# Second attention: a stack with mask rows of its own for the row maxima, in place of mask products

## The chip, the cores and the metric

The program runs on one core of a Trainium2 chip. The metric is the device time of one execution, in microseconds. The kernel before took 1235.64 us, the median of three runs (1232.64 to 1238.71).

## The reference, cut to what matters

x has 4 batches of 1024 tokens and 256 channels. Four stages add to it: an attention over 77 context rows, a gated mixture with a log, a second attention over the same context rows, and a self attention over 1024 keys in two classes. Only the third is touched:

```
n = layernorm(x)
q = n.reshape(4, 1024, 16, 16) @ Wq.T          # 16 heads of 16
k = ctx.reshape(4, 77, 16, 16) @ Wk.T
energy = einsum('bqhd,bkhd->bhqk', q, k)
energy = where(mask, energy, -1e20)            # mask: 1024 x 77, the same for all batches and heads
attn = softmax(energy / 4)                     # over the 77 keys
x = x + tanh(g) * ((attn @ v) @ Wo.T + bo)
```

The softmax needs the largest energy of each query row. The kernel computes it ahead of the scores, in a product of its own.

## The kernel before, in words

The second attention is cut into 16 units: unit u is batch u // 4 and heads 4 (u % 4) to 4 (u % 4) + 3, with 1024 tokens. A unit has two half units (m = 2u and 2u + 1) of 512 tokens, a half unit four steps (j = 0 to 3).

Precision comes from splitting queries and keys into three bf16 parts (high, middle, low). Chunks of 512 normalised tokens are split on chip and written to DRAM (`x_parts`, `write_half`, `write_parts`); then SP loads them back as a stack: 16 rows (the 16 channels of a head) for each pair of parts, 6 pairs, so 96 rows, for four heads and 1024 tokens. One such load (L553) has 128 KB, 16 rows x 4 x 1024; a unit has six. Keys are stacked the same way (`K1s`, L540). A product of stack and key stack is then the sum over all six pairs of parts.

For each unit:

- `max_product1` (L1424 to L1429) makes, for 128 queries at a time (eight per unit), the energies of four heads against 77 keys: first one mask product (L1424, the mask `mb1` against `I4`, 308 columns), then four small products of 96 rows and 77 columns (L1426). VectorE takes the negated maximum over the keys (L2028). The products use two banks in turn, so product n waits for the reduction of n - 2.
- `max_transposes1` (L1439) turns the maxima into a row; ScalarE (L1065) and GpSimd (`max_rows1`, L833) copy it under the stack as rows 96 to 99.
- `scores1` (L1459, L1460) makes keys x 512 tokens for one head, with the maxima subtracted by these rows, and adds the mask by a second product. ScalarE takes the exponential (L1085).
- `values1` (L1468) multiplies with the values, ScalarE copies (L1071), TensorE transposes back (L1477), VectorE divides (`normalise1`, L2047 and L2050).

The order is written out by hand. Step j of the scores of unit u stands behind the maxima product of unit u + 1 for the same j. So unit u + 1's stack must have landed when unit u's scores begin. In eight half units (m = 4, 6, ... 18) a half chunk of tokens is also transposed (L1380), cast by ScalarE (L1027), and its residue taken by VectorE (L1996) between two pairs of reductions; GpSimd makes the last part (L823, L825). Chunks 4 to 7 are written to `x_parts` (L545) while units 5, 7, 9 and 11 are loaded.

All transfers are issued by SP, in one queue. `load_x_stack(u)` waits until the scores of unit u - 3 are done, since three stacks are kept in turn; units 4, 8 and 12 (first of a batch) also wait until the chunks of their batch have landed in DRAM.

VectorE makes the mask `mb1` (L2005, 77 keys x 1024 tokens) from its bytes during the second stage.

Of the kernel before, what the change touches and what calls it, by code (L numbers as in the profile page):

```python
# [12 lines left out]
BF16 = mybir.dt.bfloat16  # L13
# [25 lines left out]
def build_program(nc, ins, out):  # L39
    ctx = ExitStack()  # L40
    with ctx:
# [177 lines left out]
        def parts_of(c):  # L219
# [3 lines left out]
        Xs = [v.bitcast(BF16).rearrange("p (j n) -> p j n", j=4)  # L223
              for v in (R4[0:SR1, 0:2048], R5[0:SR1, 0:2048], R5[0:SR1, 2048:4096])]
# [41 lines left out]
        STACK_DMAS = 6  # L266
# [161 lines left out]
        QM_ORDER, KM_ORDER, CLS_ROW, MROWS = (0, 0, 1), (0, 1, 0), 48, 50  # L428
# [72 lines left out]
        def _(sp):  # L501
# [36 lines left out]
            sp.dma_start(M1u, ins["mask1T"]).then_inc(s_m1, 16)  # L538
            for n, p in enumerate(K_ORDER):
                sp.dma_start(K1s[16 * n:16 * n + 16],  # L540
                             KXP[p].rearrange("(h d) n -> d h n", d=D)).then_inc(s_k1s, 16)
# [6 lines left out]
            def load_x_stack(u):  # L548
                b, hg = u // 4, u % 4
                if u >= 3:  # L550
                    sp.wait_ge(s_sc, 8 * (u - 2))
                for n, p in enumerate(Q_ORDER):
                    sp.dma_start(Xs[u % 3][16 * n:16 * n + 16],  # L553
                                 XP[p, 64 * hg:64 * hg + 64, S * b:S * b + S]
                                 .rearrange("(j d) t -> d j t", d=D)).then_inc(s_xs[u % 3], 16)
# [8 lines left out]
            sp.wait_ge(s_kw, 48)  # L564
            load_x_stack(0)
            sp.wait_ge(s_pl, 4)
            for c in range(2):
                write_half(c, 1, s_pw[c])
            for u in range(1, UNITS):
                b = u // 4  # L570
                if u % 4 == 0 or u == 2:
                    sp.wait_ge(s_pw[0], 16 * (b + 1))
                    sp.wait_ge(s_pw[1], 16 * (b + 1))
                load_x_stack(u)
                for c in WRITES.get(u, ()):
                    write_parts(c)
# [177 lines left out]
        def _(pool):  # L754
# [55 lines left out]
            pool.wait_ge(s_v1m, 8)  # L810
            pool.wait_ge(s_w1, 16 * 28)
# [17 lines left out]
            def max_rows1(m):  # L829
# [3 lines left out]
                pool.tensor_copy(Xs[m // 2 % 3][SR:SR1, :, 512 * (m % 2):512 * (m % 2) + 512],  # L833
# [15 lines left out]
            for m in range(2 * UNITS):  # L849
# [5 lines left out]
                if m + 2 < 2 * UNITS:  # L855
                    max_rows1(m + 2)
                if m == 9:
                    ln_rstd(2, [3])
                    pool.wait_ge(s_rs, 2 * 3 * B)
# [332 lines left out]
        def _(pe):  # L1192
# [218 lines left out]
            pe.wait_ge(s_k1s, 16 * STACK_DMAS)  # L1411
            pe.wait_ge(s_v1m, 8)
            pe.wait_ge(s_mk1, 1)
# [29 lines left out]
            def scores1(m):  # L1443
                u, q = m // 2, m % 2
                b, hg = u // 4, u % 4
                pe.wait_ge(s_mrc, m + 1)
                for j in range(4):
# [11 lines left out]
                    pe.matmul(o, K1s[:, 4 * hg + j, KX * b:KX * b + KX], Xs[u % 3][:, j, t], start=True, stop=False)  # L1459
# [355 lines left out]
        def _(dve):  # L1815
# [189 lines left out]
            dve.tensor_scalar(mb1, M1u, -1.0, BIG, ALU.add, ALU.mult).then_inc(s_mk1, 1)  # L2005
            add_log(2)
# [47 lines left out]
            for n in range(4, FIRST):  # L2054
                residue(n, bank(n))
            maxima1(1)
            dve.wait_ge(s_x2, NC)
            for m in range(2 * UNITS):
# [3 lines left out]
                if m in CHUNKS:  # L2062
                    ln_chunks(2, [CHUNKS[m]], lambda c: None)
                if m in STATS:
# [309 lines left out]
```

## Time and profile before

| | |
|---|---|
| median of 3 runs | 1235.64 us |
| profiled execution | 1233.77 us |
| its span | 1232.0 us |
| mean granted TensorE clock | 0.982 |
| TensorE, VectorE, ScalarE, GpSimd busy | 95%, 79%, 66%, 21% |
| 16 DMA engines busy (queue q1) | 39.6% |

The span is the time from the first to the last instruction of the profiled execution. The second attention takes from about 188 to 348 us of it; the self attention takes most of the rest. A busy TensorE counts matmuls that overlap, so starts tell more than durations. In a timeline a row merges neighbours of one kind: x4 means four of them, and the time in brackets is idleness just before, with what ended it.

### The profile page before, as it was taken

What the parts mean: (1) busy time and instruction counts of PE and PEld (TensorE: products, weight loads), DVE (VectorE), ACT (ScalarE), POOL (GpSimd) and SP (SyncE); (2) the same over time, 40 slices, a digit from 0 to 9 for tenths busy, and PEclk for the clock granted to TensorE, in tenths of its full rate; (3) what the DMA queues carried; (4) which work ended last, traced back from release to release, by engine and by line L of the source; (5) the groups of instructions that cost most, each with busy time, mean ns of one, the idle gap of its engine ahead of it and who ended that gap; (6) DMA issues with size and microseconds to landing.
All of it is one profiled execution on the core that took longest, in us unless ns stands there. A gap on an engine that the chain in (4) does not pass through costs nothing.

```text
span 1232.0 us, 26174 instructions
## 1 busy us (share of the span) xinstructions
PE 1164.6 (95%) x10391; PEld 534.3 (43%) x10391; DVE 973.2 (79%) x1431; ACT 818.4 (66%) x1471; POOL 258.3 (21%) x200
## 2 busy tenths in 40 slices
PE   5899999999998999789999999999999999999997
PEld 3577675555576456333322332332232323333345
DVE  6995587665447659688999999999999999999902
ACT  3234576777732743228888888888888888888871
POOL 3131345656632423540000000100100001001000
PEclk9978999999999999979999999999999999999999
DMA  6000336665300334751543454445534545364014
GB/s 208 25 1 17 34 78 149 108 130 104 52 27 13 116 128 120 148 77 46 91 71 71 98 98 68 90 77 94 85 79 91 98 76 92 66 100 81 12 44 142
DMA packets 89993, 101.73 MB, mean 83 GB/s; under 512 B 22154, under 2 KB 60300, under 8 KB 89872
## 3 DMA queue, kind: packets, MB, share of 16 engines
q1 hardware_dynamic: 89872, 100.06, 39.6%
q8 instruction: 83, 1.36, 0.5%
q14 instruction: 38, 0.31, 0.1%
HBM read 71.47 MB, written 24.33 MB: 78 GB/s over the span
## 4 chain that ended last, share of the span: by engine, by line
PE 60%; DVE 31%; ACT 4%; issue 2%; DMA 1%; SPq 1%; POOL 0%; POOLq 0%; ACTq 0%; DVEq 0%
DVE sm L2257 23%; PE ps L1705 11%; PE ps L1696 9%; PE ps L1683 7%; PE ps L1468 3%; PE ps L1565 3%; PE ps L1459 2%; PE ps L1460 2%; PE ps L1766 2%; PE ps L1524 2%; PE ps L1477 1%; PE ps L1426 1%; PE ps L1424 1%; ACT W L1162 1%; PE ps L1289 1%
## 5 line engine op out<-in xcount | busy, mean ns | idle before, releaser
L2257 DVE TENSOR_REDUCE sm<-ps 128x1 f32<-128x1024 f32 x512 | 601.8, 1218 | 34.8 <-PE ps L1683 30.6
L1162 ACT ACTIVATE W<-ps 128x512 f32<-128x512 f32 x1024 | 534.9, 603 | 122.6 <-PE ps L1705 120.2
L1705 PE MATMUL ps<-R 99*32 99x512 bf16 x4096 | 317.6, 384 | 0.9
L1696 PE MATMUL ps<-W,R 128*32 128x512 f32 x2048 | 265.4, 594 | 0.0
L1705 PEld LDWEIGHTS ps<-R 99*32 99x32 bf16 x4096 | 85.0, 94 | 203.6 <-ACT W L1162 156.1
L1683 PE MATMUL ps<-R 50*128 50x512 bf16 x512 | 91.6, 394 | 11.8 <-DVE sm L2257 7.5
L1683 PE MATMUL ps<-KM,R 50*128 50x512 bf16 x512 | 88.7, 384 | 5.1 <-DVE sm L2257 0.2
L1085 ACT ACTIVATE R<-ps 77x512 f32<-77x512 f32 x128 | 75.2, 593 | 20.6 <-PE ps L1460 11.3
L904 POOL COPY R<-R 128x512 f32<-128x512 f32 x16 | 9.8, 613 | 371.6 <-PE ps L1696 371.6
L1696 PEld LDWEIGHTS ps<-W,R 128*32 128x32 f32 x2048 | 63.0, 111 | 45.8 <-issue 0.5
L833 POOL COPY R<-R 4x2048 bf16<-4x2048 bf16 x32 | 60.5, 1892 | 57.0 <-ACT R L1065 49.0
L2028 DVE TENSOR_REDUCE small<-ps 128x4 bf16<-128x308 f32 x128 | 57.2, 472 | 13.3 <-PE ps L1426 13.3
L923 POOL TENSOR_TENSOR R<-R,W 128x512 f32<-128x512 f32 x8 | 10.3, 1282 | 268.0 <-DMA W<-sum_factors 268.0
L1683 PEld LDWEIGHTS ps<-R 50*128 50x128 bf16 x512 | 23.3, 93 | 98.6 <-issue 58.4
L1683 PEld LDWEIGHTS ps<-KM,R 50*128 50x128 bf16 x512 | 23.3, 93 | 95.7 <-issue 64.8
L1565 PE MATMUL ps<-R,W 128*128 128x512 f32 x128 | 58.5, 600 | 0.0
L1459 PE MATMUL ps<-R 100*77 100x512 bf16 x128 | 49.0, 383 | 0.0
L1460 PE MATMUL ps<-R 77*77 77x512 bf16 x128 | 48.6, 380 | 0.0
L1841 DVE TENSOR_SCALAR XN<-X,mv,rstd 128x256 f32<-128x256 f32 x128 | 47.0, 433 | 1.0 <-PE ps L1228 0.7
L2047 DVE RECIPROCAL small<-ps 128x16 f32<-128x16 f32 x32 | 8.2, 258 | 42.4 <-PE ps L1477 42.4
L1426 PEld LDWEIGHTS ps<-R 96*128 96x128 bf16 x512 | 33.9, 97 | 12.4
L1426 PE MATMUL ps<-R 96*128 96x77 bf16 x512 | 38.9, 198 | 0.0
(261 smaller groups left out, 1466.9 us busy)
## 6 DMA issues: line engine op xcount, KB each, us to landing
R<-x_parts SPq DMA_DIRECT2D x96, 128.0 KB, 4.6
R<-q_parts SPq DMA_DIRECT2D x192, 64.0 KB
R<-q_parts SPq DMA_DIRECT2D x96, 128.0 KB
R<-k_parts SPq DMA_DIRECT2D x96, 128.0 KB
q_parts<-R SPq DMA_DIRECT2D x24, 256.0 KB, 2.6
k_parts<-R SPq DMA_DIRECT2D x24, 256.0 KB, 2.7
x_parts<-R SPq DMA_DIRECT2D x6, 768.0 KB, 4.2
X<-in_x SPq DMA_DIRECT2D x4, 1024.0 KB, 10.2
```

What stands on the lines that cost most here:

```text
L833: pool.tensor_copy(Xs[m // 2 % 3][SR:SR1, :, 512 * (m % 2):512 * (m % 2) + 512], mrow1[:, m % 2].unsqueeze(1).to_broadcast([4, 4, 512])).t ...
L1085: act.activation(P1[:, m % 2, j, :], score_bank1(n)[0:KX, :], ACT.Exp, scale=0.25).then_inc(s_e1, 1)
L1162: act.activation(PR[:, s % 2, h, :], third_bank("score", 64 * u + n), ACT.Exp, scale=0.25).then_inc(s_sfree, 1)
L1426: mm = pe.matmul(o[:, KX * j:KX * j + KX], Xs[u % 3][0:SR, j, P * q:P * q + P], K1s[0:SR, 4 * hg + j, KX * b:KX * b + KX], start=False, st ...
L1459: pe.matmul(o, K1s[:, 4 * hg + j, KX * b:KX * b + KX], Xs[u % 3][:, j, t], start=True, stop=False)
L1460: pe.matmul(o, I4[:, 0:KX], mb1[:, t], start=False, stop=True).then_inc(s_sc, 1)
L1565: mm = pe.matmul(o[:, 512 * j:512 * j + 512], wqkv[:, i, C * kind + P * j:C * kind + P * j + P], XNT3[:, i, 512 * c:512 * c + 512], start= ...
L1683: mm = pe.matmul(pl[:, 512 * i:512 * i + 512], QMH[j][h][v, P * q:P * q + P], KM[j][v, h, :], start=True, stop=True)
L1696: mm = pe.matmul(bank(7)[32 * h:32 * h + 32, :], VST[j][:, k, h, :], PR[:, s % 2, h, :], start=(k == 0), stop=(k == TB - 1))
L1705: mm = pe.matmul(o[32 * c:32 * c + 32, :], KST[j][0:MAX_ROW + 1, h, t:t + 32], QST[j][0:MAX_ROW + 1, h, 512 * (s // 8):512 * (s // 8) + 51 ...
L2028: dve.tensor_reduce(Mn[:, u % 2, q, :], bank(n % 2)[:, 0:4 * KX].rearrange("p (j n) -> p j n", j=4), AX, ALU.max, negate=True).then_inc(s_ ...
L2257: dve.tensor_reduce(MX[:, half, h, q:q + 1], bank(2 * ((p + 1) % 2), 2), AX, ALU.max).then_inc(s_tfree, 1)
```

## The change

The maxima get stacks and key stacks of their own. A maxima stack has 125 rows: 77 mask rows (`mb1`, repeated for four heads) and 3 x 16 part rows, for the part pairs (0,0), (0,1) and (1,0) instead of all six. The maxima's key stack has a 77 x 77 identity over the key parts. One product of 125 rows then holds both mask and energies, and the product with `I4` is gone. The scores keep their stack of 96 + 4 rows.

The mask rows stay in place while part rows below them are loaded anew: even units use one buffer, odd units another (units 13 and 15 a third), so VectorE writes the mask rows three times (`mask_rows1`). GpSimd writes the identity four times (`preset_max_keys1`). SP loads three part groups per unit ahead of the six of the scores, three key groups per batch, and the wait counts change (`group_loads`).

```
+        def group_loads(g):
+            return 16 * sum((MAX_DMAS if n < UNITS else 0) + (STACK_DMAS if n else 0) for n in range(g % 3, g + 1, 3))
...
+            load_max_keys1(0)
             for n, p in enumerate(K_ORDER):
                 sp.dma_start(K1s[16 * n:16 * n + 16],
...
+            def load_max_stack1(u):
+                b, hg = u // 4, u % 4
+                if u == 2:
+                    sp.wait_ge(s_mp, 8)
+                if u >= 3:
+                    sp.wait_ge(s_sc, 8 * (u - 2))
+                if u == 13:
+                    sp.wait_ge(s_pl, 2 * NC)
+                for n, p in enumerate(QM_ORDER):
+                    sp.dma_start(max_stack1(u)[KX + 16 * n:KX + 16 * n + 16],
                                  XP[p, 64 * hg:64 * hg + 64, S * b:S * b + S]
                                  .rearrange("(j d) t -> d j t", d=D)).then_inc(s_xs[u % 3], 16)
...
+            load_max_stack1(0)
             load_x_stack(0)
+            sp.wait_ge(s_dl, NC)
+            load_max_stack1(1)
...
             for u in range(1, UNITS):
                 b = u // 4
                 if u % 4 == 0 or u == 2:
                     sp.wait_ge(s_pw[0], 16 * (b + 1))
                     sp.wait_ge(s_pw[1], 16 * (b + 1))
+                if u >= 2:
+                    load_max_stack1(u)
                 load_x_stack(u)
+                if u == 2:
+                    sp.wait_ge(s_k1s, 16 * (MAX_DMAS + STACK_DMAS))
+                    for n in range(1, B):
+                        load_max_keys1(n)
                 for c in WRITES.get(u, ()):
                     write_parts(c)
...
             def max_product1(u, qs):
                 b, hg = u // 4, u % 4
-                pe.wait_ge(s_xs[u % 3], 16 * STACK_DMAS * (u // 3 + 1))
+                pe.wait_ge(s_xs[u % 3], group_loads(u))
+                pe.wait_ge(s_mk1, 4 if u >= 13 else 3 if u >= 1 else 2)
+                if b >= 1:
+                    pe.wait_ge(s_k1s, 16 * (MAX_DMAS * B + STACK_DMAS))
+                    pe.wait_ge(s_v1m, 9 + b)
                 for q in qs:
                     n = 8 * u + q
                     if n >= 2:
                         pe.wait_ge(s_mr, n - 1)
                     o = bank(n % 2)[:, 0:4 * KX]
-                    pe.matmul(o, mb1[:, P * q:P * q + P], I4, start=True, stop=False, skip_group_check=True)
                     for j in range(4):
-                        mm = pe.matmul(o[:, KX * j:KX * j + KX], Xs[u % 3][0:SR, j, P * q:P * q + P],
-                                       K1s[0:SR, 4 * hg + j, KX * b:KX * b + KX], start=False, stop=True,
+                        mm = pe.matmul(o[:, KX * j:KX * j + KX], max_stack1(u)[:, j, P * q:P * q + P],
+                                       max_keys1(b)[:, 4 * hg + j, :], start=(j == 0), stop=True,
                                        skip_group_check=True)
...
+            def mask_rows1(u):
+                dve.tensor_copy(max_stack1(u)[0:KX], mb1.unsqueeze(1).to_broadcast([KX, 4, S])).then_inc(s_mk1, 1)
+
+            dve.wait_ge(s_mk1, 1)
+            dve.wait_ge(s_kw, 16)
+            mask_rows1(0)
```

The load of the scores' stack now waits on the semaphore of the next unit's group (`s_xs[(u + 1) % 3]`), so the maxima products of a unit wait for their own three loads and for the six of the unit before.

TensorE, one half unit of the second attention without a transposed half, before (L1424 is the mask product, L1426 the small ones, L1459 and L1460 the scores):

```order
187 L1424 MATMUL ps<-R 128x308
188 L1426 MATMUL ps<-R 128x77 x4
189 L1459 MATMUL ps<-R 77x512
190 L1460 MATMUL ps<-R 77x512
191 L1424 MATMUL ps<-R 128x308
192 L1426 MATMUL ps<-R 128x77 x4
193 L1459 MATMUL ps<-R 77x512
194 L1460 MATMUL ps<-R 77x512
```

The same place after (L1490 the small products, L1525 and L1526 the scores):

```order
147 L1490 MATMUL ps<-R 128x77 x4
148 L1525 MATMUL ps<-R 77x512
149 L1526 MATMUL ps<-R 77x512
150 L1490 MATMUL ps<-R 128x77 x4
151 L1525 MATMUL ps<-R 77x512
152 L1526 MATMUL ps<-R 77x512
```

The products of 308 columns are gone; nothing else moved there. SP's queue from the first stack on, before (L553 loads for the scores' stack, L558 and L545 writes of parts):

```order
29 L558 DMA x_parts<-R 128x3x512 x2
30 L553 DMA R<-x_parts 16x4x1024 x6
31 L558 DMA x_parts<-R 128x3x512 x2
32 L553 DMA R<-x_parts 16x4x1024 x12
33 L545 DMA x_parts<-R 128x6x512 x2
34 L553 DMA R<-x_parts 16x4x1024 x18
35 L545 DMA x_parts<-R 128x6x512
```

And after (L594 loads for the maxima's stack, L581 for the scores', L562 keys of the maxima, L599 and L573 writes):

```order
30 L599 DMA x_parts<-R 128x3x512 x2
31 L594 DMA R<-x_parts 16x4x1024 x3
32 L581 DMA R<-x_parts 16x4x1024 x6
33 L594 DMA R<-x_parts 16x4x1024 x3
34 L599 DMA x_parts<-R 128x3x512 x2
35 L581 DMA R<-x_parts 16x4x1024 x6
36 L594 DMA R<-x_parts 16x4x1024 x3
37 L581 DMA R<-x_parts 16x4x1024 x6
38 L562 DMA W<-ctx_key_parts 16x16x77 x9
39 L573 DMA x_parts<-R 128x6x512 x2
40 L594 DMA R<-x_parts 16x4x1024 x3
```

Every unit now has nine stack loads. Unit 2's three maxima loads and nine key loads stand ahead of the writes of chunks 2 and 3. VectorE, at the mask and before the first maxima, after (L2071 makes the mask, L2074 is the new copy, L2101 the reductions, L2062 the residues):

```order
102 L2034 TENSOR_TENSOR R<-R 128x1024
103 L2071 TENSOR_SCALAR R<-R 77x1024
104 L2074 COPY R<-R 77x4096
105 L2039 SCALAR_TENSOR_TENSOR X<-R,gates,X 128x1024
...
122 L2101 TENSOR_REDUCE small<-ps 128x4 x4
123 L2062 TENSOR_TENSOR R<-ps,R 128x512 x4
124 L2074 COPY R<-R 77x4096
125 L2101 TENSOR_REDUCE small<-ps 128x4 x8
```

The copies are new; their neighbours stand as before.

## Rows read from the trace of the kernel before

**Rows 1.** The page, busy time of the engines.
```profile
PE 1164.6 (95%) x10391; PEld 534.3 (43%) x10391; DVE 973.2 (79%) x1431; ACT 818.4 (66%) x1471; POOL 258.3 (21%) x200
```

**Rows 2.** Chain of waits in order of time, 278 to 310: start us, us, what.
```profile
279.39 0.99 PE ps L1468 x8
...
284.48 1.00 PE ps L1468 x8
...
289.15 1.00 PE ps L1468 x8
```

**Rows 3.** Timeline of TensorE where unit 2's scores begin.
```profile
211.95 0.30 PE L1424 MATMUL ps<-R 77*128 77x308 bf16 x1
212.09 0.30 PE L1426 MATMUL ps<-R 96*128 96x77 bf16 x4
```

**Rows 4.** Loads of one stack line L553, units 8 and 9, each by itself.
```profile
L553 SPq DMA_DIRECT2D R<-x_parts x6: 302/426/427, 253.2 to 255.4; - x6
DMA to landing us min/median/max: 3.2/4.7/6.0
...
L553 SPq DMA_DIRECT2D R<-x_parts x6: 302/427/1734, 259.2 to 262.7; - x6
DMA to landing us min/median/max: 3.3/4.2/4.6
```

**Rows 5.** Windows: span, busy of each engine, clock, DMA share, GB/s.
```profile
302.50:304.50 2.00, 2.00 (x21) 0.81 (x20) 0.52 (x2) 1.45 (x3) 1.94 (x2) 1.00 1.04 124
190.00:192.00 2.00, 1.61 (x18) 1.06 (x19) 2.00 (x4) 1.16 (x3) 0.48 (x1) 1.00 1.04 182
```

**Rows 6.** Timeline, first maxima product of unit 8.
```profile
261.51 0.29 PE L1424 MATMUL ps<-R 77*128 77x308 bf16 x1 [0.53 <-issue]
```

**Rows 7.** Timeline, outputs' transposes, first reductions, third mask product of a half unit.
```profile
304.33 0.65 PE L1477 MATMUL ps<-identF,R 128*128 128x128 f32 x4
...
305.65 0.85 DVE L2028 TENSOR_REDUCE small<-ps 128x4 bf16<-128x308 f32 x2
...
306.27 0.29 PE L1424 MATMUL ps<-R 77*128 77x308 bf16 x1
```

**Rows 8.** Timeline, end of a half unit with a transposed half.
```profile
274.60 0.85 DVE L2028 TENSOR_REDUCE small<-ps 128x4 bf16<-128x308 f32 x2
...
275.51 0.24 PEld L1439 LDWEIGHTS ps<-identB,small 128*4 128x4 bf16 x4 [0.70 <-DVE small L2028]
```

**Rows 9.** Groups by line and form, VectorE: busy us, mean ns.
```profile
L1928 DVE CAST R<-small 128x3072 bf16<-128x3072 f32 x1 | 1.8, 1761 | 0.0
```

**Rows 10.** Timeline of VectorE, behind the mask and at unit 0's last reductions.
```profile
158.04 1.28 DVE L1973 SCALAR_TENSOR_TENSOR X<-R,gates,X 128x1024 f32<-128x1024 f32 x1 [0.52 <-ACT R L1017]
...
193.73 0.86 DVE L2028 TENSOR_REDUCE small<-ps 128x4 bf16<-128x308 f32 x2 [0.23 <-PE ps L1426]
```

**Rows 11.** Timeline of TensorE, beginnings of the scores of units 0 and 15.
```profile
194.97 0.30 PE L1424 MATMUL ps<-R 77*128 77x308 bf16 x1
...
337.55 0.38 PE L1459 MATMUL ps<-R 100*77 100x512 bf16 x1
```

**Rows 12.** Writes of chunks 2 and 3 (L545): issue to landing.
```profile
DMA to landing us min/median/max: 4.2/4.2/4.2
```

**Rows 13.** Loads of the key stack, line L540.
```profile
L540 SPq DMA_DIRECT2D R<-ctx_key_parts x6: 330/448/449, 140.6 to 142.9; - x6
DMA to landing us min/median/max: 3.4/5.8/7.6
```

**Rows 14.** Windows around a stop of TensorE after the second attention.
```profile
396.00:399.00 3.00, 0.82 (x8) 0.00 (x0) 3.00 (x5) 1.93 (x3) 2.13 (x1) 1.00 0.00 0
399.00:402.50 3.50, 3.01 (x10) 2.43 (x11) 3.50 (x7) 1.90 (x3) 0.00 (x0) 0.52 0.65 225
```

**Rows 15.** Loads of unit 2's stack (L553), issued behind others.
```profile
L553 SPq DMA_DIRECT2D R<-x_parts x6: 303/424/557, 186.5 to 188.8; - x6
DMA to landing us min/median/max: 3.6/4.5/4.9
```

More of the change, by code:

```diff
@@ L222, in build_program, with x_stack, max_stack1, max_keys1 @@
         xres = R4[:, 2048:4096].rearrange("p (u j n) -> p u j n", u=2, j=2)
-        Xs = [v.bitcast(BF16).rearrange("p (j n) -> p j n", j=4)
-              for v in (R4[0:SR1, 0:2048], R5[0:SR1, 0:2048], R5[0:SR1, 2048:4096])]
+        QM_ORDER, KM_ORDER = (0, 0, 1), (0, 1, 0)
+        def x_stack(u):
+            v = (R4[0:SR1, 0:2048], R5[0:SR1, 0:2048], R1[0:SR1, 4096:6144] if u == 2 else R2f[0:SR1, 0:2048])[u % 3]
+            return v.bitcast(BF16).rearrange("p (j n) -> p j n", j=4)
+        MAXR = KX + 48
+        def max_stack1(u):
+            v = R5[0:MAXR, 2048:4096] if u % 2 == 0 else R1[0:MAXR, 6144:8192] if u < 12 else R4[0:MAXR, 2048:4096]
+            return v.bitcast(BF16).rearrange("p (j n) -> p j n", j=4)
+        def max_keys1(b):
+            v = R2f[0:MAXR, 7482:8098] if b == 0 else W[0:MAXR, 2048 + 616 * b:2664 + 616 * b]
+            return v.bitcast(BF16).rearrange("p (h n) -> p h n", h=H)
         On = R1[:, :].rearrange("p (i c) -> p i c", i=NT)
@@ L538, in _, with load_max_keys1 @@
             sp.dma_start(M1u, ins["mask1T"]).then_inc(s_m1, 16)
+            def load_max_keys1(b):
+                for n, p in enumerate(KM_ORDER):
+                    sp.dma_start(max_keys1(b)[KX + 16 * n:KX + 16 * n + 16],
+                                 KXP[p].rearrange("(h d) n -> d h n", d=D)[:, :, KX * b:KX * b + KX]
+                                 ).then_inc(s_k1s, 16)
+            load_max_keys1(0)
             for n, p in enumerate(K_ORDER):
@@ L810, in _, with preset_max_keys1 @@
             pool.wait_ge(s_v1m, 8)
+            def preset_max_keys1(b):
+                pool.tensor_copy(max_keys1(b)[0:KX], identB[0:KX, 0:KX].unsqueeze(1).to_broadcast([KX, H, KX])
+                                 ).then_inc(s_v1m, 1)
+            preset_max_keys1(0)
             pool.wait_ge(s_w1, 16 * 28)
@@ L832, in max_rows1 @@
                     pool.wait_ge(s_sc, 4 * (m - 5))
-                pool.tensor_copy(Xs[m // 2 % 3][SR:SR1, :, 512 * (m % 2):512 * (m % 2) + 512],
+                if m == 10:
+                    for n in range(2):
+                        pool.wait_ge(s_pw[n], 32)
+                pool.tensor_copy(x_stack(m // 2)[SR:SR1, :, 512 * (m % 2):512 * (m % 2) + 512],
                                  mrow1[:, m % 2].unsqueeze(1).to_broadcast([4, 4, 512])).then_inc(s_mrc, 1)
@@ L856, in _ @@
                     max_rows1(m + 2)
+                if m in (1, 3, 4):
+                    pool.wait_ge(s_dl, NC)
+                    preset_max_keys1((m + 1) // 2 if m < 4 else 3)
                 if m == 9:
@@ L1410, in _ @@
             keep_warm(3, 4)
[L1411 to L1413 removed]
+            pe.wait_ge(s_k1s, 16 * (MAX_DMAS + STACK_DMAS))
+            pe.wait_ge(s_v1m, 9)
             pe.wait_ge(s_v1c, 2)
@@ L1446, in scores1 @@
                 pe.wait_ge(s_mrc, m + 1)
+                if u + 1 == UNITS:
+                    pe.wait_ge(s_xs[UNITS % 3], group_loads(UNITS))
                 for j in range(4):
@@ L1457, in scores1 @@
                     t = slice(512 * q, 512 * q + 512)
-                    pe.matmul(o, K1s[:, 4 * hg + j, KX * b:KX * b + KX], Xs[u % 3][:, j, t], start=True, stop=False)
+                    pe.matmul(o, K1s[:, 4 * hg + j, KX * b:KX * b + KX], x_stack(u)[:, j, t], start=True, stop=False)
                     pe.matmul(o, I4[:, 0:KX], mb1[:, t], start=False, stop=True).then_inc(s_sc, 1)
@@ L2055, in _ @@
                 residue(n, bank(n))
+            dve.wait_ge(s_dl, NC)
+            mask_rows1(1)
             maxima1(1)
@@ L2063, in _ @@
                     ln_chunks(2, [CHUNKS[m]], lambda c: None)
+                if m == 21:
+                    dve.wait_ge(s_pl, 2 * NC)
+                    mask_rows1(13)
                 if m in STATS:
```

8 lines of the change are left out of this document (5 added, 3 removed).

## The prediction

> **What bounds the kernel now.** I read the page first: TensorE is busy 95% of the span [rows 1], and about 150 of its 1232.0 us are the second attention, the only stage that the change touches. Then the chain of waits in order of time over that stage. It runs through TensorE alone: the value products (L1468) that close a half unit start 5.09 us apart where a half of 512 tokens is transposed inside the half unit, and 4.67 us apart where none is [rows 2]. So here a column less on TensorE is time saved, as long as nothing else becomes late. The timeline of TensorE gives the price of a mask product: L1424 starts at 211.95, the first small product behind it at 212.09 [rows 3]: 0.14 us, though its own duration is 0.30 (it is pipelined). There are 128 of them: 128 x 0.14 = 17.9 us is the most that their removal can return.
>
> The views of the transfers come last, and they decide. The six loads of unit 8's query stack are issued from 253.2 to 255.4; the first lands 3.2 us after its issue (256.4), the last 6.0 us after its own (261.4) [rows 4]. Five loads in 5.0 us: 1.0 us for each load of 128 KB, though SP issues one every 0.45 us. Unit 9's six are issued from 259.2 to 262.7 and have landed by 267.3 [rows 4]: twelve loads, still 1.0 us each. In such a stretch the 16 DMA engines are busy all the time (share 1.04) at only 124 GB/s [rows 5]. A unit of two half units has 6 us of such loads in 9.35 us, so they hide; with nine it has 9. And the queue is late once already: TensorE starts the first mask product of unit 8 at 261.51, after 0.53 us of idleness [rows 6], just behind the landing at 261.4. That is the wait that grows.
>
> **Removed.** The 128 mask products. In a half unit without a transposed half, the fourfold gain of 0.14 (0.56 us) is not got in full. VectorE normalises first: transposes of the outputs at 304.33, first reduction at 305.65 (+1.32), 0.47 long, and the third product of the half unit waits for its bank: +1.85. TensorE comes there at +1.94 now (306.27) [rows 7], and would come at +1.65. So it waits 0.2 us there, and the gain is 0.35. With a transposed half inside, the chain transposes, ScalarE cast, VectorE residue, two reductions has no slack even now: the reductions end at 275.45 (274.60 + 0.85) and the next loads of TensorE follow at 275.51 [rows 8]. That chain starts only 0.28 us earlier and then queues behind ScalarE's exponentials; I take 0.15. Over half units 0 to 29: eight at 0.15, nineteen at 0.35, the first three at about 0.5: 9.4 us. The units of the maxima then last 9.3 us (units 2 to 9) and 8.7 us (from 10).
>
> **Added, before the first unit.** VectorE writes 77 mask rows of 4096 bf16 elements three times. No row shows such a copy. The cast of L1928 takes 1.76 us for 3072 elements [rows 9], 0.57 ns each: 2.35 us is the upper end. It moves 6 bytes an element and the copy 4; by bytes it is 1.57, which I take; were it twice as fast as the cast, 1.2. The first copy stands between L2005 and L1973, where VectorE is idle 0.52 us [rows 10]; what follows to the start of the stage is one chain of VectorE, ScalarE and TensorE, so 1.05 us is lost. The second stands before the reductions that the last two products of unit 0 wait for: 1.57. The prologue's own products give back 0.3. The third, late in unit 10, fits VectorE's idle time. Scores begin at 194.97 now [rows 11], then at 197.3. [...] GpSimd's four presets of 77 x 1232 elements fall into its idle time.
>
> **Added, in SP's queue.** Three loads more a unit, of the same form and size (16 rows x 4 x 1024). They stand ahead of the six, and SP issues them when the unit three before has been scored. Also nine loads of key parts (39 KB each) ahead of the writes of chunks 2 and 3. The writes of parts stand behind the loads of their unit as before, and at units 4, 8 and 12 SP waits until the writes have landed before it loads anything. Prices:
> a load 1.0 us; its landing after an idle queue 3.2 (so 2.2 of start). A write of 768 KB lands 4.2 us after its issue [rows 12]: 2.0 of its own beyond the start; I take 2.5, since it stands behind loads. Key loads: the nearest row is the key stack, 154 KB in packets of 616 B: first landing 3.4 after 140.6, last 7.6 after 142.9 [rows 13], so 1.3 us each. By bytes a quarter of it, 0.33; by number of packets (the same 256), 1.3. I take 0.33, as they queue behind loads that are already issued: 3.0 for nine.
>
> The ledger, in the trace's time. Unit 0's last product ends near 194.0 now (the last pair of its reductions starts at 193.73 [rows 10]), at 196.4 then; its buffer is unit 2's, so SP issues unit 2's maxima stack only then: landed 196.4 + 2.2 + 3 = 201.6 (needed 204). Unit 2's query stack 207.6, keys 210.6, two writes 215.6, unit 3's maxima stack 218.6. Its products stand in unit 2's scores, which begin at 211.95 now [rows 3] and could begin at 212.5: **a stop of 6.1 us**. It is the largest single term. From then on the beginnings of the units are the later of TensorE's (the one before + 9.3 or 8.7) and of the queue's: unit 3 227.9 (TensorE), 4 237.2 (TensorE), 5 248.1 (queue, behind write 4), 6 257.4, 7 270.8 (queue: unit 7's loads end at 263.1, write 5 at 265.6, then 5.2 for unit 8's maxima stack), 8 280.1, 9 291.3 (queue), 10 300.6, 11 314.0 (queue, behind write 7), 12 323.0, 13 332.0, 14 341.0 (all queue, 9 loads each), 15 349.6. Unit 15 begins at 337.55 now [rows 11]. So **the stage ends 12.0 us later**: 9.4 gained, 2.3 paid before it, 19.3 in new waits for loads (6.1 at unit 2, 4.1 and 4.7 at units 7 and 11, the rest 1.6, 1.9 and three of 0.3).
>
> [...]
>
> [...]
>
> **Sum.** The profiled execution took 1233.77 us. 1233.8 + 12.0 = **1245.8 us**. The median of the three runs (1235.64) lies 1.9 above it, within their own spread of 6; I don't add it.
>
> **Rivals.**
> 1. Loads that pack. The six loads issued from 186.5 to 188.8 land between 3.6 and 4.9 after issue (190.1 to 193.7) [rows 15], 0.73 us each, at 182 GB/s [rows 5]; others were queued ahead of them, writes too. Were all like this, unit 2 would begin at 215.4 (stop 2.9), no later unit would wait, and unit 15 would begin at 215.4 + 8 x 9.3 + 5 x 8.7 = 333.3: 4.3 us gained, **1229.5**. Against it: units 8 and 9, twelve loads in a row at 1.0 us [rows 4]. Between the two ends (12.0 us later at 1.0, 4.3 earlier at 0.73) the sign turns near 0.88 us a load. Chance 0.13.
> 2. Halfway, 0.9 us a load. By the same ledger only unit 2 (stop 4.9) and units 7 and 11 (1.2 and 2.9) wait: unit 15 begins 1.7 us later than now, **1235.5**. Chance 0.22.
> 3. Small packets and writes cost more: keys 1.3 each (+8.7 at unit 2, whose delay the full queue passes on): **1254.5**. Chance 0.13.
> 4. The change does what it says on TensorE; the order of instructions shows the mask products gone.
> My forecast: 0.52, its own range 1240 to 1253.
>
> Half a percent, 6.2 us, is about what a measurement can tell. Slower by more (over 1241.8): most of the forecast (0.49), rival 3 and a little of rival 2: 0.64. Faster by more (under 1229.5): half of rival 1 and a part more if VectorE's waits are smaller than I think: 0.10. The same: 0.26. Range: 1230 to 1256.
>
> **What would show it.** In the timeline of the changed kernel: TensorE idle 5 to 7 us at the first product of unit 3; waits of 2 to 5 us where units 8 and 12 are first needed; landings still 1.0 us apart and DMA share near 1 in the whole stage; units of 9.0 us at its end. Wrong if the landings come 0.75 apart, if the steps without a transposed half go down to 4.1 us, or if TensorE is busy throughout.

## The result and the profile after

The changed kernel took 1250.12 us, the median of 13 runs (1245.86 to 1253.76); the kernel before took 1236.76 us in 13 runs beside it (1232.3 to 1244.44). The ratio is 1.0099, 95% interval 1.0081 to 1.0116, so 12.2 us slower (10.0 to 14.3). The forecast was 12.0 us slower. As a time it was 1245.8, 4.3 below the median, since the 12.0 were added to a single execution of 1233.8. The difference is right; the runs below show that it came out right from parts of which several were wrong.

The profiled execution of the changed kernel took 1250.54 us, 16.8 more than the one of before. So differences between these two traces are 3 to 5 us larger than those between medians; most of that is found below (the clock at 37 to 44 us).

The page, busy time of the engines; it answers to [rows 1]:

```profile
PE 1162.0 (93%) x10263; PEld 528.0 (42%) x10263; DVE 984.3 (79%) x1434; ACT 816.2 (65%) x1471; POOL 267.8 (21%) x204
```

TensorE has 128 instructions fewer and waits more. The chain of waits in order of time, the value products that close a half unit (start us, us, what), answers to [rows 2]:

```profile
278.38 1.00 PE ps L1534 x8
...
283.01 0.99 PE ps L1534 x8
...
287.60 0.99 PE ps L1534 x8
```

4.63 and 4.59 us, where before it was 4.67 and 5.09: a unit is 0.55 us shorter. And the chain stays on TensorE: here no wait for a load. The timeline of TensorE (start us, us, what, in brackets the idle time just before) has two stops and no third:

```profile
227.06 0.42 PE L1490 MATMUL ps<-R 125*128 125x77 bf16 x4 [7.60 <-issue]
...
316.98 0.31 PE L1490 MATMUL ps<-W,R 125*128 125x77 bf16 x4 [3.69 <-DVE small L2101]
```

The first is the forecast one: unit 3's first product, inside unit 2's scores ([rows 3] is that place before). It waits for unit 3's maxima stack, issued from 217.1, the last part landed at 227.0. The second was not forecast. It stands in unit 11's scores, at the products for unit 12, and belongs to VectorE, whose third copy is at the end of its own half unit 21, in unit 10. VectorE and GpSimd at that time:

```profile
310.23 4.52 POOL L926 TENSOR_TENSOR X<-X,bo 128x2048 f32<-128x2048 f32 x1
310.31 5.52 DVE L2074 COPY R<-R 77x4096 bf16<-77x4096 bf16 x1
...
314.80 2.77 POOL L892 COPY R<-R 4x2048 bf16<-4x2048 bf16 x1
315.75 0.24 DVE L2120 RECIPROCAL small<-ps 128x16 f32<-128x16 f32 x1
```

The third mask copy begins 0.08 us after GpSimd's bias add and ends 1.1 us after it. The three copies together, by their line:

```profile
L2074 DVE COPY R<-R x3: 1223/1848/5522, 161.2 to 310.3; 77x4096 bf16<-77x4096 bf16 x3
```

1.22, 1.85 and 5.52 us for the same work. Beside the first stands GpSimd's power of the variances (L828). At this place it took 1.67 us in the kernel before, and 3.86 here:

```profile
159.59 1.60 POOL L826 TENSOR_SCALAR rstd<-mv 128x8 f32<-128x8 f32 x1 [5.14 <-DVE mv L2048]
161.27 3.86 POOL L828 TENSOR_TENSOR rstd<-rstd,mhalf 128x8 f32<-128x8 f32 x1
```

VectorE at that time:

```profile
161.18 1.22 DVE L2074 COPY R<-R 77x4096 bf16<-77x4096 bf16 x1
162.32 1.27 DVE L2039 SCALAR_TENSOR_TENSOR X<-R,gates,X 128x1024 f32<-128x1024 f32 x1
```

The copy ends at 162.4 and the power only at 165.1, 1.5 us after the instruction behind the copy (L2039). So the 2.2 us look like both: the copy began 0.09 us before the power, and L2039 came straight behind it. In the kernel before the power began first, 0.34 us ahead of the same instruction [rows 10], and took 1.67. The next power, at 180.90, took 2.53 us beside L2039 alone; it did so in run 1 too, which has no copy.

The second copy, too, ends 1.1 us after the GpSimd instruction beside it (201.4 and 200.3). The first took 1.22 us in all, so the second and the third look as if they had waited for GpSimd and copied then: at the third 4.52 us of the add, then 1.1 us of copying. That is a reading of two places; in run 2 the copy has no add beside it.

Windows (span, busy of PE, PEld, DVE, ACT, POOL, clock, DMA share, GB/s) of the changed kernel: in the first stage, behind the stop, and where the first copy stands:

```profile
37.00:44.00 7.00, 7.00 (x18) 5.08 (x19) 4.97 (x13) 0.46 (x2) 0.00 (x0) 0.55 0.04 2
226.00:229.00 3.00, 1.94 (x12) 1.23 (x13) 0.85 (x2) 0.57 (x1) 0.00 (x0) 0.50 1.06 156
158.00:172.00 14.00, 9.55 (x46) 8.23 (x45) 11.28 (x27) 6.97 (x10) 5.45 (x2) 0.88 0.00 1
```

and of the kernel before:

```profile
37.00:44.00 7.00, 7.00 (x28) 4.30 (x27) 6.96 (x20) 0.27 (x2) 0.00 (x0) 1.00 0.04 4
158.00:172.00 14.00, 11.70 (x62) 9.95 (x61) 12.75 (x29) 10.91 (x16) 5.28 (x4) 1.00 0.00 1
```

In 37 to 44 us both kernels run the same instructions, but the changed one's granted clock was 0.55, and before 1.00. VectorE's instructions behind it come 3.6 us later. Of the ten kernels below, all alike there, five show 0.53 to 0.62 in their profile (runs 1, 3, 8, 9, 10) and five 1.00, with the change and without it: I take it for a difference between executions and no effect of the change. Take it off, and the traces differ by 13.2 us, close to the medians.

The table splits the difference of the two traces. "Start" is the first value product, "end" the last.

| part | predicted | between the traces |
|---|---|---|
| stage starts later | 2.3 | 7.8, of which 3.6 the clock at 37 to 44 us |
| stop at unit 3's first product | 6.1 | 7.6, and 2.6 in the slow clock behind it |
| later waits for loads | 13.2 | 0 |
| third copy, in unit 10 | 0 | 6.5 (a stop of 3.7, and 2.8 in the slow clock behind it) |
| gain by the missing products | -9.4 | -8.0 |
| sum | 12.0 to 12.2 | 16.5 |

(The half unit with the stop took 14.81 us where its neighbours of that kind take 4.59; the two with the copy 8.55 and 6.79 in place of 4.43 each. The gain is what is left of 16.5 - 7.8 = 8.7: 10.2 and 6.5 lost, 8.0 gained. The granted clock was 0.50 from 222 to 232 us, which begins within the first stop, and from 318 to 324.)

### The profile page after: what moved, and what is told of

Same layout as the page of the kernel before. It is cut to its first block, busy times and chain, and to the rows that moved or that the text cites. A ratio compares the mean times of both kernels' runs of the same rounds, so it can differ in the third digit from the quotient of the medians.

```text
span 1248.8 us, 26114 instructions
## 1 busy us (share of the span) xinstructions
PE 1162.0 (93%) x10263; PEld 528.0 (42%) x10263; DVE 984.3 (79%) x1434; ACT 816.2 (65%) x1471; POOL 267.8 (21%) x204
## 4 chain that ended last, share of the span: by engine, by line
PE 58%; DVE 32%; ACT 4%; issue 3%; DMA 1%; POOL 1%; SPq 1%; POOLq 0%; ACTq 0%; DVEq 0%
DVE sm L2335 23%; PE ps L1771 11%; PE ps L1762 9%; PE ps L1749 7%; PE ps L1534 2%; PE ps L1631 2%; PE ps L1525 2%; PE ps L1526 2%; PE ps L1832 2%; PE ps L1490 2%; PE ps L1590 2%; PE ps L1543 1%; PE ps L1326 1%; PE ps L1351 1%; ACT W L1224 1%
## 5 line engine op out<-in xcount | busy, mean ns | idle before, releaser
L2101 DVE TENSOR_REDUCE small<-ps 128x4 bf16<-128x308 f32 x128 | 57.5, 473 | 15.3 <-PE ps L1490 10.5
L985 POOL TENSOR_TENSOR R<-R,W 128x512 f32<-128x512 f32 x8 | 10.2, 1276 | 270.2 <-DMA W<-sum_factors 270.2
L1525 PE MATMUL ps<-R 100*77 100x512 bf16 x128 | 50.5, 394 | 0.0
L1526 PE MATMUL ps<-R 77*77 77x512 bf16 x128 | 50.3, 393 | 0.0
L1490 PEld LDWEIGHTS ps<-W,R 125*128 125x128 bf16 x384 | 25.3, 100 | 24.8 <-issue 13.1
L1490 PE MATMUL ps<-W,R 125*128 125x77 bf16 x384 | 30.4, 201 | 5.6 <-DVE small L2101 3.7
```

The source lines that it names most:

```text
L1490: mm = pe.matmul(o[:, KX * j:KX * j + KX], max_stack1(u)[:, j, P * q:P * q + P], max_keys1(b)[:, 4 * hg + j, :], start=(j == 0), stop=True ...
L1525: pe.matmul(o, K1s[:, 4 * hg + j, KX * b:KX * b + KX], x_stack(u)[:, j, t], start=True, stop=False)
L1526: pe.matmul(o, I4[:, 0:KX], mb1[:, t], start=False, stop=True).then_inc(s_sc, 1)
L2101: dve.tensor_reduce(Mn[:, u % 2, q, :], bank(n % 2)[:, 0:4 * KX].rearrange("p (j n) -> p j n", j=4), AX, ALU.max, negate=True).then_inc(s_ ...
```

## The experiments

Ratios are to the kernel before, run beside them, with 95% intervals; 1% is 12.4 us.

**1. The gain alone.** The kernel before with one line less:

```
-                    pe.matmul(o, mb1[:, P * q:P * q + P], I4, start=True, stop=False, skip_group_check=True)
...
-                                       K1s[0:SR, 4 * hg + j, KX * b:KX * b + KX], start=False, stop=True,
+                                       K1s[0:SR, 4 * hg + j, KX * b:KX * b + KX], start=(j == 0), stop=True,
```

> The kernel before with its 128 mask products left out (the maxima are taken over unmasked energies); loads, stacks and all else as before. It prices the gain on TensorE alone. Theory A (the prediction's step): VectorE, not TensorE, sets the third product of a half unit, so 0.35 us come back in a half unit without a transposed half and 0.15 in one with it, 9.4 us in all: about 1227.4. Theory B (what the trace of the changed kernel suggests): 0.55 us a unit while halves are transposed, 0.24 a half unit afterwards, about 7.5 us: 1229. Rival C: every product is worth its 0.14 us, 17.9 us: 1219.

1230.59 us, ratio 0.9960 (0.9939 to 0.9981): 4.9 us faster (2.3 to 7.5). In its trace the half units take 4.57 and 4.63 us in turn, then 4.41; from the first value product to the last the stage is 136.3 us long where it was 143.7. That is 7.4 us, near the 7.5 of theory B and at the upper end of what the times allow; rival C is out, and so is the 9.4 of theory A. So about 40% of the 17.9 us of the products' own time comes back in the stage.

**2. The third copy without GpSimd's add beside it.**

```
-                if m in (20, 23, 26, 29):
-                    b = (m - 20) // 3
+                if m in (22, 24, 26, 28):
+                    b = (m - 22) // 2
```

> The changed kernel with GpSimd's four bias adds moved from half units 20, 23, 26, 29 to 22, 24, 26, 28; VectorE's third mask copy stays in half unit 21. Theory A: the copy took 5.52 us because it waited for the add that GpSimd had begun 0.08 us earlier (4.52 us long); without it the copy takes 1.2 to 1.9 us and hides, and the 5.9 us that TensorE lost there come back: about 1244.5. Rival B: the copy is slow by itself, or because stack loads fill SBUF meanwhile: it stays at 5 us and so does the time, 1250.

1245.02 us, ratio 1.0079 (1.0043 to 1.0115). VectorE's timeline at the copy, and TensorE's in unit 12:

```profile
306.38 1.21 DVE L2074 COPY R<-R 77x4096 bf16<-77x4096 bf16 x1
308.23 0.26 DVE L2120 RECIPROCAL small<-ps 128x16 f32<-128x16 f32 x1 [0.64 <-PE ps L1543]
```

```profile
322.96 0.31 PE L1490 MATMUL ps<-W,R 125*128 125x77 bf16 x4 [1.49 <-issue]
...
349.63 0.41 PE L1525 MATMUL ps<-R 100*77 100x512 bf16 x1 [1.15 <-POOL R L892]
```

The same copy takes 1.21 us and hides: the half unit is back at 4.42. That shows theory A for the mechanism, and rival B false. The time came down by 2.5 us by the ratios and 5.1 by the medians, and the intervals of the two kernels overlap; the trace shows why it is less than 5.9. Two new stops take back 1.4 and 1.3 us. The second waits for GpSimd's copy of the last row maxima, which now stands behind the moved add. The first is open: it lies in the second half of unit 12's scores, the loads that it needs had landed by 316.2 and GpSimd's rows were written at 321.6. It is not one of the waits for loads of the forecast. And before the first value product the clock was 0.50 (201 to 207 us), 2.7 us lost, so that the stop at unit 3 was only 5.17 us here, with the same loads.

**3. Key loads behind the writes.**

```
-                if u == 2:
-                    sp.wait_ge(s_k1s, 16 * (MAX_DMAS + STACK_DMAS))
-                    for n in range(1, B):
-                        load_max_keys1(n)
                 for c in WRITES.get(u, ()):
                     write_parts(c)
+                if u == 3:
+                    sp.wait_ge(s_k1s, 16 * (MAX_DMAS + STACK_DMAS))
+                    for n in range(1, B):
+                        load_max_keys1(n)
```

> The changed kernel with the nine loads of key parts moved from behind unit 2's loads to behind unit 3's, so that they no longer stand ahead of the writes of chunks 2 and 3. In the changed kernel they landed from 214.5 to 220.0 us. Theory A: they hold the queue 4.6 us, so the stop of 7.6 us at unit 3's first product becomes 3.0, the slow clock behind it shrinks from 2.1 to about 1, and the time falls by 5 to 6 us: 1244.5. Rival B: keys cost 0.33 us each, as predicted: the stop becomes 4.6, the time 1247. Rival C: SP's issue, not the transfer, is the limit, and the nine cost the same further back, at unit 4: 1250.

1247.24 us, ratio 1.0083 (1.0066 to 1.0100). TensorE's timeline:

```profile
219.98 0.31 PE L1490 MATMUL ps<-R 125*128 125x77 bf16 x4 [0.72 <-issue]
...
233.89 0.42 PE L1490 MATMUL ps<-W,R 125*128 125x77 bf16 x4 [4.53 <-DMA R<-x_parts]
```

The stop at unit 3's first product is gone but for 0.72 us, more than theory A expected (3.0), and 4.53 us of it stand at unit 4's first product instead. The three half units that hold both stops last 21.75 us (5.47, 4.63, 11.65) where the same three last 23.95 in the changed kernel: 2.2 gained. Mostly rival C: the queue carries the same work and is full until 234 us (DMA share 1.30 in 222 to 234 us).

**4. Unit 2's query loads first.**

```
+                if u == 2:
+                    load_x_stack(u)
                 if u >= 2:
                     load_max_stack1(u)
-                load_x_stack(u)
+                if u != 2:
+                    load_x_stack(u)
```

> The changed kernel with unit 2's six query loads issued before its three maxima loads, which must wait for unit 0's last product; the six fill a buffer that is free, so they use the queue while it would stand idle from 203.2 on. Nothing else moves. Theory A: the stop at unit 3's first product is a queue of transfers begun too late; six loads of 1.0 us leave it, stop 7.6 becomes 1.5, the clock stays full, time 1250 - 8 = 1242. Rival B: the stop is the writes' own (they wait for the parts of chunk 3, made at about 204, and take 9 us from issue): stop above 5, 1248.

1243.50 us, ratio 1.0052 (1.0033 to 1.0070), 5.8 us better than the changed kernel by the ratios. The stop at unit 3 is gone, as theory A has it, but there is one of 2.12 us at unit 2's first product, since its maxima loads now stand behind six others:

```profile
208.12 0.42 PE L1493 MATMUL ps<-R 125*128 125x77 bf16 x4 [2.12 <-issue]
208.34 0.63 PE L1528 MATMUL ps<-R 100*77 100x512 bf16 x1
...
217.88 0.31 PE L1493 MATMUL ps<-R 125*128 125x77 bf16 x4
218.03 0.38 PE L1528 MATMUL ps<-R 100*77 100x512 bf16 x1
```

A score product takes 0.63 us up to 217.2 and 0.38 from 218.0; the granted clock was 0.50 in 208.1 to 217.2 us and 1.00 in 218 to 222. The two half units last 7.95 and 6.48 us in place of 3.92 and 4.43: 6.1 lost, of which 2.1 is waiting and 4.0 the clock of 0.50. By the clock a stop of 2 us cost no less here than the one of 7.6 us in the changed kernel (2.6).

**5. The early copies moved.** The first to before the fourth log sum, the second to before unit 0's first reductions.

```
-            mask_rows1(0)
             add_log(2)
...
             add_zero_factor(3)
+            mask_rows1(0)
             add_log(3)
...
+            dve.wait_ge(s_dl, NC)
+            mask_rows1(1)
             maxima1(0)
             for n in range(4, FIRST):
                 residue(n, bank(n))
-            dve.wait_ge(s_dl, NC)
-            mask_rows1(1)
             maxima1(1)
```

> The changed kernel with the first two mask copies moved into times in which VectorE waits: the first from before the third log sum to before the fourth (where GpSimd's power of the variances no longer runs beside it), the second from before unit 0's last reductions to before its first. In the changed kernel they cost 0.7 us of their own, 1.5 us through GpSimd (its power took 3.9 us beside the copy, 1.7 without it), and 1.9 us: 4.1 together. Theory A: TensorE reaches the stage 3.4 to 4.1 us earlier and the transfers, whose first ones are released by the same chain, move with it: 1246.5. Rival B: the queue is full from the loads of unit 1's stack on, so unit 3's first product starts no earlier, the stop grows by what the prologue gains, and the time stays at 1249 to 1250.

1242.46 us, ratio 1.0051 (1.0032 to 1.0070), 5.9 us better than the changed kernel; rival B is out. The copies' line, and the window in which the first stood before:

```profile
L2074 DVE COPY R<-R x3: 1216/1217/5516, 163.1 to 300.6; 77x4096 bf16<-77x4096 bf16 x3
```

```profile
158.00:172.00 14.00, 11.74 (x62) 9.97 (x61) 13.79 (x30) 10.98 (x16) 5.28 (x4) 1.00 0.00 1
```

Both early copies take 1.22 us, GpSimd's power 1.67 again. The clock in 158 to 172 us is 1.00. All six kernels with the copy there (the changed one, runs 2, 3, 4, 7 and 9) have 0.88, with 9.5 to 10.0 us of work for TensorE; of the six without it two (runs 1 and 10) have 0.88 too. So it goes with the copy at that place, but two kernels have it without a copy, and what brings it stays open. In the same eight kernels the next power of GpSimd took 2.53 us, in the four others 1.67.

This trace's stage begins 8.9 us earlier than the changed kernel's, 5.3 without the 3.6 at 37 to 44 us. What they are made of shows in the time from the power (161.27 in the changed kernel) to the first value product (209.23): 48.0 us there, 42.6 here and 43.7 in the kernel before. Without mask products and without copies it is 44.2 where that clock was 0.88 (runs 1 and 10) and 42.5 where it was 1.00 (run 8). So the clock, with the longer second power, is 1.7 us, the early copies 3.8 in the changed kernel and 0.1 in this run, and the missing products give back 1.2.

**6. All repairs together.** The copies as in run 5, the third at half unit 22, and the keys of three batches in 3 loads:

```
-                if m == 21:
+                if m == 22:
...
+                if u == 3:
+                    sp.wait_ge(s_k1s, 16 * (MAX_DMAS + STACK_DMAS))
+                    for n, p in enumerate(KM_ORDER):
+                        sp.dma_start(late_keys1[KX + 16 * n:KX + 16 * n + 16],
+                                     KXP[p].rearrange("(h d) n -> d h n", d=D)[:, :, KX:B * KX]).then_inc(s_k1s, 16)
```

> The changed kernel with all of its repairs that keep nine stack loads a unit: both early copies as in the run before, the third copy one half unit later (22, away from GpSimd's bias add), and the key parts of batches 1 to 3 loaded by 3 transfers of 115 KB in place of 9 of 39 KB, between unit 3's maxima loads and its query loads. Theory A: the third copy gives 5.9 us back, the early ones 2 to 4, and the stop of 9.7 us shrinks to about 4, since the queue still has 3 + 6 loads, two writes and 3 + 3 loads ahead of unit 4's maxima stack: 1234 to 1237, no different from the kernel before. Rival B: all pieces add up (5.9 + 4.1 + 9.7): 1230.5. Rival C: with nine loads a unit the queue is full all through the stage, and what is gained early turns into waits at units 8 and 12: 1241.

1230.47 us, ratio 0.9944 (0.9919 to 0.9970): 6.9 us faster than the kernel before (3.7 to 10.0), and 19 faster than the change as it was made. TensorE's waits for loads, all three of them:

```profile
209.95 0.31 PE L1494 MATMUL ps<-R 125*128 125x77 bf16 x4 [0.50 <-issue]
219.58 0.30 PE L1494 MATMUL ps<-W,R 125*128 125x77 bf16 x4 [0.25 <-issue]
...
293.37 0.30 PE L1494 MATMUL ps<-W,R 125*128 125x77 bf16 x4 [0.49 <-issue]
```

Rival B had the time: all pieces add up. Theory A overstated what would remain of the stop. One piece is not repaired in full: at half unit 22 the third copy meets another GpSimd instruction, takes 2.71 us and ends 1.1 after it, and TensorE waits 0.85 us.

```profile
295.58 1.89 POOL L896 COPY R<-R 4x2048 bf16<-4x2048 bf16 x1
295.85 2.71 DVE L2078 COPY R<-R 77x4096 bf16<-77x4096 bf16 x1
```

**7. Most maxima loads left out.** The changed kernel with `MAX_DMAS` counted and issued only for the units in `LOADED = (0, 1, 2, 3, 4, 13)`; the other units take their maxima from part rows of earlier units.

> The changed kernel without the maxima loads of units 5 to 12, 14 and 15 (the maxima there come from the part rows of earlier units); keys, copies and the first five units as in the changed kernel. 30 of the 48 loads of 128 KB are gone. Theory A (from the changed kernel's trace): these loads are hidden in full, since TensorE nowhere waits for them: the time stays at 1250 within 1.5. Rival B (the prediction's ledger): nine loads a unit are more than the queue can carry, and TensorE's steps are stretched by the wait at units 5, 7, 9 and 11: 1237 to 1240. Rival C: the loads slow the engines by filling SBUF beside them: half units get shorter than 4.60 and 4.43.

1249.66 us, ratio 1.0115 (1.0094 to 1.0137): no gain over the changed kernel. Half units stay at 4.59, 4.62 and 4.42. Windows of 226 to 300 us in this kernel, then in the changed one:

```profile
226.00:300.00 74.00, 72.87 (x657) 38.95 (x656) 50.04 (x129) 57.86 (x102) 45.59 (x34) 0.97 0.75 137
```

```profile
226.00:300.00 74.00, 71.90 (x644) 38.95 (x644) 49.23 (x128) 56.15 (x99) 44.51 (x34) 0.96 0.97 160
```

The DMA share falls from 0.97 to 0.75 and no half unit gets shorter. So in the changed kernel the 30 late loads were hidden in full, and they do not slow the engines either.

**8. VectorE's order.** Run 1 with the normalisation moved to between the second and third reductions:

```
+                    def between():
+                        if n is not None:
+                            residue(n, bank(2))
+                        if m >= 3:
+                            normalise1(m - 3)
+                    maxima1(m + 2, between)
```

> The kernel before without its mask products (as in the first run of this series), and VectorE's normalisation of a half unit moved from ahead of the first two reductions to between the second and the third. Theory A (the prediction's step): the third product of a half unit waits for the reduction that stands behind the normalisation; with the order changed the half units without a transposed half go from 4.41 to about 4.15 us (4.67 less 4 x 0.14), some 4 us in all: 1226.5. Rival B: the transposes of the maxima, which need the fourth reduction, then wait instead: 4.4 stays, 1230.6. Rival C: something else (ScalarE's exponentials of 0.59 us, four and two copies a half unit, 3.5 us) holds them: no change.

1229.64 us, ratio 0.9956 (0.9933 to 0.9978), no different from run 1. The mechanism is as the prediction had it: half units without a transposed half went from 4.41 to 4.13 us where nothing else is late. TensorE's value products:

```profile
294.56 1.06 PE L1467 MATMUL ps<-R,W 77*32 77x512 f32 x8
...
298.69 1.06 PE L1467 MATMUL ps<-R,W 77*32 77x512 f32 x8
...
302.82 1.07 PE L1467 MATMUL ps<-R,W 77*32 77x512 f32 x8
...
307.94 1.06 PE L1467 MATMUL ps<-R,W 77*32 77x512 f32 x8
```

4.13, 4.13, then 5.12. The gain is given back in half units that follow one with a transposed half (4.97 for 4.63) and where GpSimd adds the bias (5.12 for 4.55).

**9. The keys in three loads, alone.** The three loads of run 6, behind unit 2's query loads as the nine were; the bytes are the same.

> The changed kernel with the key parts of batches 1 to 3 loaded by 3 transfers of 115 KB (packets of 462 bytes) in place of 9 of 39 KB (packets of 154 bytes), at the same place, behind unit 2's query loads. The bytes are the same. The nine landed within 4.6 us behind the query loads, and SP took 0.55 us to issue each. Theory A: their number (packets and issues), not their bytes, was the price; the three take 2.5 to 3 us, the writes behind them are issued 3 us earlier, and the stop of 7.6 us at unit 3's first product becomes 5 to 6: 1247. Rival B: they cost by bytes, as the prediction had it: nothing changes, 1249 to 1250. Rival C: the whole 4.6 us goes: stop 3, 1244.

1245.96 us, ratio 1.0082 (1.0050 to 1.0114); the interval does not tell it from the changed kernel. The trace does:

```profile
224.07 0.42 PE L1494 MATMUL ps<-R 125*128 125x77 bf16 x4 [4.96 <-issue]
```

The three landed within 2.3 us behind the query loads, the nine within 4.6 (and within 4.5 to 4.7 in runs 2, 5 and 7, which have the nine at the same place), and the stop is 4.96 in place of 7.60 us. The landings tell it better than the stop, which was 5.17 and 4.89 in runs 2 and 5 for reasons of their own. So the number of packets or issues was half of the price (theory A); packets and issues were not told apart.

**10. That order only at the end.** As run 8, from half unit 19 on.

> The kernel before without its mask products, and the normalisation between the second and third reductions only from half unit 19 on, where no half is transposed any more. With it everywhere such half units took 4.13 us in place of 4.41, but the ones before a transposed half 4.97 in place of 4.63, and the three in which GpSimd adds the bias 5.12 in place of 4.55. Theory A: 8 x 0.28 less 3 x 0.57, so 0.5 us less than without it, no measurable difference: 1230. Rival B: the three bias adds no longer cost once VectorE is not late from the half units before: 2.3 us less, 1228.

1228.57 us, ratio 0.9946 (0.9924 to 0.9969), not to be told from run 1 or 6. The three half units with the bias add stay at 5.12 (rival B false). Its profile shows something else, at unit 8's first product:

```profile
261.76 0.30 PE L1425 MATMUL ps<-R 96*128 96x77 bf16 x4 [2.12 <-issue]
```

It stands just behind the landing of unit 8's last query load at 261.7, the place of [rows 6], where the wait was 0.53 us. The two half units around it take 5.0 us more than their like: 2.1 of waiting, and 2.9 in the slow clock that follows (0.50 in 264 to 269 us). In run 1 the same place costs 0.2 us: its stage began 4 us later, for reasons outside of it, and both end at 343.6. Run 8 waited 1.20 us there. So TensorE alone being faster can run into this wait, and part of the gain is lost there in some profiles.

## Why the prediction was right in sum, and where it was wrong

**What bounds the kernel.** Right: TensorE's steps set the stage, and queued loads are what a faster TensorE meets first (the stop at unit 3's first product; the waits of runs 9 and 10).

**Removed.** Right in mechanism, 1.4 us too high in sum: 8.0 in the trace of the changed kernel, 7.4 in run 1, forecast 9.4. Run 8 shows VectorE's normalisation as the limit where no half is transposed. The split was wrong: a step with a transposed half gains 0.50 (I had 0.15), and the one behind it nearly nothing (4.63 for 4.67, I had 0.35).

**Added before the first unit.** Wrong in size, 2.3 against about 4.2 (7.8 less 3.6): 3.8 for the copies and 1.7 for the clock of 0.88 in 158 to 172 us, less 1.2 for the missing products (forecast 2.6, nothing, and 0.3; run 5). The copies' own length was over-estimated (1.57; by itself it is 1.22). The other estimate there, 1.2 for a copy twice as fast as the cast, was the better one. What failed is the step by which the first copy costs its own length less the 0.52 us that VectorE is idle: I looked at VectorE alone. With the copy before it GpSimd's power ended 2.2 us later, and VectorE waited for that (1.57 us at 165.16).

**"The third, late in unit 10, fits VectorE's idle time."** This step failed outright too: the copy cost 6.5 us in the trace. The row that tells it was there, in GpSimd's timeline of before, just ahead of the place at which the copy was put:

```profile
298.17 4.53 POOL L864 TENSOR_TENSOR X<-X,bo 128x2048 f32<-128x2048 f32 x1
```

**The stop at unit 2's end.** Right: forecast 6.1, measured 7.6. The excess is about the keys': 4.6 us where I took 3.0. The rule "by bytes" failed, run 9 shows. The slow clock behind it (0.50 in 222 to 232 us) cost 2.6 us, for which the sum has no term, and no later wait took it up.

**The later waits for loads**, 13.2 us: none. This was the largest term of the sum, and its step failed outright: the ledger let the queue set the beginnings of units 5, 7, 9 and 11 to 14, and TensorE set them all. Loads alone do land 1.0 us apart: unit 8's maxima loads were issued from 268.4 and their last landed at 273.6. But the ledger added 2.5 us for each write to nine full loads, and it did not let loads pack behind a write: unit 6, with the write of chunk 4 among its loads, took 10.6 us from landing to landing (11.5 forecast), unit 7 8.2 (9 forecast). It also let SP issue at the beginning of the next unit's scores, and SP issues before the value products, some 1.5 us earlier (unit 7's loads from 255.4, the products at 256.98). The query loads of units 6 and 7, whose last ones landed at 258.3 and 266.5:

```profile
L581 SPq DMA_DIRECT2D R<-x_parts x6: 423/426/428, 248.6 to 251.0; - x6
DMA to landing us min/median/max: 4.7/6.0/7.3
...
L581 SPq DMA_DIRECT2D R<-x_parts x6: 425/426/428, 258.3 to 260.6; - x6
DMA to landing us min/median/max: 3.8/4.9/5.9
```

So unit 8's maxima stack was there 1.8 us before TensorE asked for it:

```profile
L594 SPq DMA_DIRECT2D R<-x_parts x3: 303/426/427, 268.4 to 269.2; - x3
DMA to landing us min/median/max: 3.2/3.9/4.5
```

```profile
275.43 0.31 PE L1490 MATMUL ps<-W,R 125*128 125x77 bf16 x4
```

Waits that are differences of two nearly equal rates (9 loads in 9.2 us) can't be had from prices known to 10%; the ledger should have entered them with a range through nothing. Run 7 settles it for this kernel. The reserve was thin at one place: unit 12's maxima stack, behind a write, landed at 311.5 in the changed kernel, 0.4 us before TensorE asked for it, and in run 9 it came late:

```profile
309.67 0.30 PE L1494 MATMUL ps<-W,R 125*128 125x77 bf16 x4 [1.18 <-issue]
```

Runs 4 and 6 waited 0.76 and 0.49 us there. It is the place for which the forecast had 4.7 us.

So 13.2 us of waits that did not come stand against 6.5 (third copy), 2.6 (clock behind the stop), 1.9 (start), 1.5 (stop) and 1.4 (gain) that were not foreseen, 13.9 in all. That the forecast lies 0.2 us from the measured difference is luck.

**Rivals.** Rival 1 (loads that pack) is right that no later unit waits, though loads by themselves still land 1.0 us apart; its gain of 4.3 us is within what the structure gives when the copies and the keys are placed well (run 6: 3.7 to 10.0). Rival 3 was right that small transfers cost more than their bytes, but it was 0.5 us for each of the nine, and it gave 1.3.

Open: why the clock at 37 to 44 us is 0.53 to 0.62 in some profiles and 1.00 in others; what brings the clock of 0.88 in 158 to 172 us; what held TensorE at 322.96 in run 2; and whether the number of packets or SP's issue made the nine key loads dear.

## What to carry to other kernels

Before an instruction is put into an engine's idle time, read the timelines of the other engines at that very place too: a VectorE copy of 1.2 us took 5.5 beside a GpSimd add of 4.5, and cost TensorE 6.5. Count each moved or added transfer in the stretch where the queue is full, here the 30 us in which the first three units start, by number as well as by bytes: 30 loads of 128 KB later on cost nothing. Where a mask or bias only serves a shift that the result does not depend on, as the row maximum in a softmax, leaving it out of the maximum (run 1) gave as much, within the intervals, as the whole rebuilt structure (run 6). That holds as long as masked energies do not exceed the others by so much that the exponentials vanish.

## What the runs showed of the hardware

- A VectorE copy of 77 x 4096 bf16 elements takes 1.22 us, 0.30 ns an element, against 0.57 for the cast from float32 [rows 9]; beside a GpSimd instruction it took 1.85, 2.71 (run 6) and 5.52 us, and each time it ended 1.1 us after that instruction. GpSimd was late beside VectorE too: its power of 1.67 us took 3.86 where a copy of 1.22 us and an instruction of 1.27 (L2039) ran beside it, and 2.53 beside such an instruction alone (run 1, at 180.62).
- Behind a stop of TensorE of 2.12 us the granted clock was 0.50 in run 4 (208.1 to 217.2 us, 4.0 us more lost) and in run 10 (264 to 269 us, 2.9 more). In the changed kernel it was 0.50 behind the stop of 3.69 us (318 to 324 us, 2.8 more) and behind the one of 7.60 (222 to 232 us, 2.6 more). Behind the stop of 1.90 us ahead of unit 0's scores it was 0.50 in run 2 (201 to 207 us, 2.7 us lost), but 1.00 in the changed kernel and in runs 3, 4, 7 and 9, which have the same stop.
- Nine loads of 39 KB in packets of 154 bytes took 4.6 us in the changed kernel, three of 115 KB in packets of 462 bytes 2.3 in run 9.
